# Attention state kept per half of a sequence, outputs as rounded high and low products, and level scores of two blocks in alternation

## The reference, cut to what matters

```
x = h @ up_w.T ; shift = silu(conv4(x)) ; q, k, g, tau = projections of shift
v = sigmoid(x @ ig_w1.T @ ig_w2.T + ig_b2) * x
it = softplus(g)**sigmoid(tau) ; rt_log = -softplus(g) * sigmoid(tau)
kn = k / max(|k|, 1e-12) * it
# for tokens t:  S_t = diag(exp(rt_log_t)) S_(t-1) + kn_t^T v_t ;  o_t = q_t S_t
o = scan(q / 8, kn, v, rt_log) + shift * residual_weight
xg = o * silu(h @ gate_w.T) ; o = xg * rsqrt(mean(xg*xg) + eps) * norm_weight
return o @ down_w.T
```

## Time and profile before

| what | value |
|---|---|
| median of 3 runs | 2241.48 us (2240.04 to 2248.97) |
| span of the profiled execution | 2240.6 us |
| PE busy | 2160.7 us, 96% of the span, 17266 matmul records |
| PEld (weight loads) | 2042.4 us, 91% |
| DVE busy | 1544.0 us, 69%, 4162 instructions |
| ACT busy | 1197.9 us, 53%, 2399 instructions |
| POOL busy | 92.0 us, 4% |
| mean granted TensorE clock | 0.997 of 2.4 GHz |
| DMA | mean 16 GB/s; near idle after the first slice of 40 |

### The profile page before, as it was taken

How to read it: one execution, slowest core, us unless ns; L and a number is a source line. 1 busy time by engine, 2 the same in 40 slices (tenths; PEclk the granted TensorE clock), 3 DMA queues, 4 the chain that set the end, 5 groups by cost and what they waited for, 6 DMA issues and landing times.

```text
span 2240.6 us, 46115 instructions
## 1 busy us (share of the span) xinstructions
PE 2160.7 (96%) x17266; PEld 2042.4 (91%) x17266; DVE 1544.0 (69%) x4162; ACT 1197.9 (53%) x2399; POOL 92.0 (4%) x103
## 2 busy tenths in 40 slices
PE   1999999999999999999999999999999999999999
PEld 1999989999899998999989899998999989999998
DVE  6777667777667676666766677776767766667665
ACT  5565545555455564455645455554555545556453
POOL 0000000000000000000000000000000000000000
PEclk9999999999999999999999999999999999999999
DMA  7000000000000000000000000000000000000000
GB/s 272 1 11 11 11 12 1 11 11 11 12 6 6 12 11 12 11 2 11 11 12 11 7 6 11 11 11 12 1 11 12 11 11 11 1 11 11 11 6 6
DMA packets 23441, 34.96 MB, mean 16 GB/s; under 512 B 2946, under 2 KB 19714, under 8 KB 23187
## 3 DMA queue, kind: packets, MB, share of 16 engines
q1 hardware_dynamic: 23186, 31.46, 4.2%
HBM read 23.07 MB, written 8.39 MB: 14 GB/s over the span
## 4 chain that ended last, share of the span: by engine, by line
PE 95%; issue 3%; SPq 0%; ACT 0%; DVE 0%; DMA 0%; POOL 0%; POOLq 0%; DVEq 0%; ACTq 0%
PE fb L316 59%; PE ab L316 17%; PE ab L487 4%; PE ab L500 4%; PE ab L503 3%; PE ab L508 3%; PE ab L438 1%; PE ab L428 1%; PE ab L366 1%; PE ab L480 1%; PE fb L549 0%; ACT wwhole L597 0%; SPq L225 0%; DMA small<-stage_w 0%; PE ab L478 0%
## 5 line engine op out<-in xcount | busy, mean ns | idle before, releaser
L316 PE MATMUL fb<-hid1h,wwhole 128*128 128x256 f32 x2048 | 501.8, 286 | 0.0
L316 PE MATMUL fb<-hid1l,wwhole 128*128 128x256 f32 x2048 | 488.1, 279 | 0.0
L316 PE MATMUL fb<-hid0l,wwhole 128*128 128x256 f32 x2048 | 483.8, 279 | 0.0
L316 PE MATMUL fb<-hid0h,wwhole 128*128 128x256 f32 x2048 | 483.8, 279 | 0.0
L697 ACT ACTIVATE raw<-fb,sh_s 128x256 f32<-128x256 f32 x512 | 213.6, 468 | 449.6 <-PE fb L316 345.7
L316 PEld LDWEIGHTS fb<-hid1h,wwhole 128*128 128x128 f32 x2048 | 384.0, 187 | 56.3 <-issue 51.9
L316 PEld LDWEIGHTS fb<-hid1l,wwhole 128*128 128x128 f32 x2048 | 384.3, 188 | 0.0
L316 PEld LDWEIGHTS fb<-hid0h,wwhole 128*128 128x128 f32 x2048 | 384.1, 188 | 0.0
L316 PEld LDWEIGHTS fb<-hid0l,wwhole 128*128 128x128 f32 x2048 | 384.1, 188 | 0.0
L997 DVE SCALAR_TENSOR_TENSOR shift<-shift,resw_s,ab 128x128 f32<-128x128 f32 x256 | 71.9, 343 | 267.0 <-PE ab L503 202.5
L316 PE MATMUL fb<-xnth,wwhole 128*128 128x256 f32 x1024 | 239.3, 277 | 0.0
(11 more groups left out here) (179 smaller groups left out, 4472.4 us busy)
## 6 DMA issues: line engine op xcount, KB each, us to landing
xin<-x SPq DMA_DIRECT2D x32, 256.0 KB, 2.7
out<-xin SPq DMA_DIRECT2D x32, 256.0 KB, 2.3
stream<-stage_w SPq DMA_DIRECT2D x6, 512.0 KB, 7.2
sgate<-stage_w SPq DMA_DIRECT2D x4, 512.0 KB, 4.3
shift<-stage_w SPq DMA_DIRECT2D x4, 512.0 KB, 5.2
v<-stage_w SPq DMA_DIRECT2D x4, 512.0 KB, 5.5
raw<-stage_w SPq DMA_DIRECT2D x3, 512.0 KB, 6.0
mixed<-stage_w SPq DMA_DIRECT2D x3, 512.0 KB, 8.4
```

What stands on the lines that cost most here:

```text
L316: mm = pe.matmul(o, a, b, start=start and i == 0, stop=stop and i == len(pairs) - 1)
```

## The change

The state is no longer updated after each block of 128 tokens but once per sequence, at the end of the first half, and it is read once, in the second half. What the second block of a half needs of the first comes as a "cross" score block of 128x128 (`atth[:, 1, :]`), a product of `kx` (decayed k of block 0) with the decayed q of block 1. So the outputs of a half are one set of products: v of block 0 with [own scores | cross scores] (256 columns), v of block 1 with its own scores (128 columns), and in the second half the state with the decayed q of both blocks (256 columns).

All operands of these products are now split: ScalarE writes the high parts of v (`vh`, in the place of `parth`), of the cross block, of the decayed k (`kdh`), of the scores (`atth`) and of the state (`stateh`), VectorE the low parts. The products are fp32r with 128 rows. The state products take `qhl`, which has the high part of q in rows 0 to 63 and the low part in rows 64 to 127, against a state that is held twice.

The norms block gets a second product with `pair_ones` (the sum of q*k, `qk_sum`) in the place of `own`; the transposes run in first halves only. The level scores of both blocks are issued together, block 0 and block 1 in turn, ahead of h2; the break in the middle of h2's first tile is gone. Both output sets are issued after quarter b = 2, in first halves behind the state update. On VectorE both `masked` come together, the third quarter of `hidden_low` behind them and the fourth behind the seven additions.

The diff, cut to its core (most of the lines that it removes are left out here; they stand in the listing above):

```diff
+        atth, attl = sb("atth", [P, 3, CH], F32R), sb("attl", [P, 3, CH], F32R)
+        stateh, statel = sb("stateh", [P, DI], F32R), sb("statel", [P, DI], F32R)
+        kdq = sb("kdq", [P, 2, N], F32R)
+        kdh, kdl = (kdq[:, i, :].rearrange("p (c a k) -> p c a k", c=NC, a=2) for i in range(2))
+        qhl = kdq[:, 0, :]
...
+        kx, qs = bsum[rows(1), :], small[rows(0), 4:6, :]
...
@@ tensor engine @@
-                            if name == "h2" and m == 0 and k == FB // 2:
-                                level_scores(1)
...
                 pe.wait_ge(qk_ev.sem, qk_ev.at(me))
                 pe.wait_ge(tanh_d.sem, tanh_d.at(me, 2))
+                pe.wait_ge(score_d.sem, score_d.at(me))
+                if p == 0:
+                    pe.transpose(ab[2][:, 0:P], t5, ident_s[:]).then_inc(kt_mm.sem, 1)
                 pe.matmul(ab[3][:, N:N + NC], t4, pair_ones[:], start=True, stop=True)
...
+                pe.matmul(ab[3][:, N + NC:N + 2 * NC], qk, pair_ones[:], start=True, stop=True)
+                pe.matmul(ab[3][:, 0:CH], kx, t1[rows(1), :], start=True, stop=True).then_inc(dg_mm.sem, 1)
+
+                pe.wait_ge(v_d.sem, v_d.at(me))
+                pe.wait_ge(levq_d.sem, levq_d.at(me))
+                pe.wait_ge(levk_d.sem, levk_d.at(me))
+                for i in range(LEVELS):
+                    for c in range(NC):
                         mm = pe.matmul(ab[c][:, i * UP:(i + 1) * UP], lev[rows(c), i, :], levq[rows(c), i, :], start=True, stop=True)
+                mm.then_inc(lv_mm.sem, 1)
+
+                def state_update():
...
+                    pairs = []
+                    for c in range(NC):
+                        hi, lo = (t[:, c, :, :].rearrange("p a k -> p (a k)") for t in (kdh, kdl))
+                        pairs += [(hi, vh[:, c, :]), (hi, vl[:, c, :]), (lo, vh[:, c, :])]
+                    wide(ab[3][:], pairs).then_inc(su_mm.sem, 1)
+
+                def outputs():
...
                     for d in range(DB):
+                        o = ab[d // 2][:, (d % 2) * N:(d % 2 + 1) * N]
+                        cols = slice(d * P, (d + 1) * P)
+                        first = [(vh[:, 0, cols], atth[:, 0:2, :]), (vh[:, 0, cols], attl[:, 0:2, :]), (vl[:, 0, cols], atth[:, 0:2, :])]
+                        if p == 1:
+                            first += [(stateh[:, cols], qhl), (statel[:, cols], qhl)]
+                        wide(o, first, stop=False)
+                        mm = wide(o[:, CH:N], [(vh[:, 1, cols], atth[:, 2, :]), (vh[:, 1, cols], attl[:, 2, :]),
+                                               (vl[:, 1, cols], atth[:, 2, :])], start=False)
+                        if d % 2 == 1:
+                            mm.then_inc(ot_mm.sem, 1)
                 for b in range(4):
                     pe.wait_ge(gelu1_d.sem, gelu1_d.at(me, 2 * b + 2))
                     hidden("h2", b, hid1h, hid1l, h2_mm, hid1_hi, hid1_lo)
-                    if b in (1, 2):
-                        outputs(b - 1)
+                    if b == 2:
+                        if p == 0:
+                            state_update()
+                        outputs()
...
@@ scalar engine @@
+                act.wait_ge(v_d.sem, v_d.at(me))
+                act.activation(vh, v[:], ACT.Copy).then_inc(vhi_d.sem, 1)
...
+                if p == 1:
+                    act.wait_ge(qs_d.sem, qs_d.at(seq))
+                    act.activation(qhl[rows(0), :].rearrange("p (c t) -> p c t", c=NC), qs, ACT.Copy).then_inc(q_hi.sem, 1)
...
+                act.activation(atth[:, 1, :], ab[3][:, 0:CH], ACT.Copy, scale=rkn[:, 0:1]).then_inc(cross_hi.sem, 1)
+                if p == 0:
+                    for c in range(NC):
+                        act.activation(kdh[:, c, :, :], ab[2][:, c * K:(c + 1) * K].unsqueeze(1).to_broadcast([P, 2, K]), ACT.Copy,
+                                       scale=rkn[:, c:c + 1]).then_inc(kd_hi.sem, 1)
...
+                    if b == 0:
+                        act.wait_ge(att_d.sem, att_d.at(me))
+                        act.activation(atth[:, 0:3:2, :], att[:], ACT.Copy).then_inc(att_hi.sem, 1)
+                    if b == 2 and p == 0:
+                        act.wait_ge(su_mm.sem, su_mm.at(seq))
+                        act.activation(stateh[:], ab[3][:], ACT.Copy).then_inc(st_hi.sem, 1)
...
@@ vector engine @@
-                dve.tensor_tensor(t5, k_s, t5, ALU.mult).then_inc(kd_d.sem, 1)
+                dve.tensor_tensor(kx, k_s[rows(0), :], t5[rows(0), :], ALU.mult).then_inc(kx_d.sem, 1)
                 dve.tensor_tensor(t1, q_s, t1, ALU.mult).then_inc(qd_d.sem, 1)
+                if p == 0:
+                    dve.tensor_tensor(qk, q_s, k_s, ALU.mult)
+                    dve.wait_ge(kx_d.sem, kx_d.at(me))
+                    dve.scalar_tensor_tensor(t5, k_s, later_k[:], t5, ALU.mult, ALU.mult).then_inc(score_d.sem, 1)
+                else:
+                    dve.tensor_tensor(qk, q_s, k_s, ALU.mult).then_inc(score_d.sem, 1)
+                    dve.wait_ge(qd_d.sem, qd_d.at(me))
+                    dve.tensor_scalar(qs[:, 0, :], t1[rows(0), :], 1.0, None, ALU.mult)
+                    dve.tensor_scalar(qs[:, 1, :], t1[rows(1), :], earlier_q[rows(1), :], None, ALU.mult).then_inc(qs_d.sem, 1)
...
                 def masked(c):
-                    dve.wait_ge(lv_mm.sem, lv_mm.at(me, c + 1))
+                    dve.wait_ge(lv_mm.sem, lv_mm.at(me))
                     dve.scalar_tensor_tensor(mprod[:, c, :, :].rearrange("p l u -> p (l u)"), ab[c][:, 0:LEVELS * UP], rkn[:, c:c + 1],
                                              masks_s[:].rearrange("p l u -> p (l u)"), ALU.mult, ALU.mult).then_inc(mask_d.sem, 1)
                 hidden_low(hid1l, hid1h, 0, hid1_hi, hid1_lo)
+                dve.wait_ge(vhi_d.sem, vhi_d.at(me))
+                low(vl, v[:], vh).then_inc(vlo_d.sem, 1)
+                if p == 1:
+                    dve.wait_ge(q_hi.sem, q_hi.at(seq))
+                    low(qhl[rows(1), :].rearrange("p (c t) -> p c t", c=NC), qs,
+                        qhl[rows(0), :].rearrange("p (c t) -> p c t", c=NC)).then_inc(q_lo.sem, 1)
                 dve.wait_ge(dg_mm.sem, dg_mm.at(me))
+                dve.tensor_copy(qk_sum[:], ab[3][:, N + NC:N + 2 * NC])
                 dve.tensor_scalar(ssk[:], ab[3][:, N:N + NC], KEPS2, None, ALU.max).then_inc(ss_d.sem, 1)
                 hidden_low(hid1l, hid1h, 1, hid1_hi, hid1_lo)
+                dve.wait_ge(ss_d.sem, ss_d.at(me))
                 dve.wait_ge(rkn_d.sem, rkn_d.at(me))
                 for c in range(NC):
-                    dve.scalar_tensor_tensor(att[:, c, :], own(c), rkn[:, c:c + 1], ident_s[:], ALU.mult, ALU.mult).then_inc(att_d.sem, 1)
+                    dve.tensor_scalar(att[:, c, :], ident_s[:], rkn[:, c:c + 1], qk_sum[:, c:c + 1], ALU.mult, ALU.mult).then_inc(att_d.sem, 1)
                 masked(0)
+                masked(1)
                 hidden_low(hid1l, hid1h, 2, hid1_hi, hid1_lo)
-                hidden_low(hid1l, hid1h, 3, hid1_hi, hid1_lo)
-                masked(1)
+                dve.wait_ge(cross_hi.sem, cross_hi.at(me))
+                dve.scalar_tensor_tensor(attl[:, 1, :], ab[3][:, 0:CH], rkn[:, 0:1], atth[:, 1, :].bitcast(F32), ALU.mult,
+                                         ALU.subtract).then_inc(cross_lo.sem, 1)
+                if p == 0:
+                    dve.wait_ge(kd_hi.sem, kd_hi.at(seq))
+                    for c in range(NC):
+                        dve.scalar_tensor_tensor(kdl[:, c, :, :], ab[2][:, c * K:(c + 1) * K].unsqueeze(1).to_broadcast([P, 2, K]),
+                                                 rkn[:, c:c + 1], kdh[:, c, :, :].bitcast(F32), ALU.mult, ALU.subtract).then_inc(kd_lo.sem, 1)
                 dve.wait_ge(mask_d.sem, mask_d.at(me))
                 for i in range(LEVELS):
                     m = CH >> (i + 1)
                     dve.wait_ge(att_d.sem, att_d.at(me, NC + i))
                     upper = att[:].rearrange("p c (b u r) -> p c b u r", u=2, r=m)[:, :, :, 1, :]
                     dve.tensor_tensor(upper, upper, mprod[:, :, i, :].rearrange("p c (b r) -> p c b r", r=m), ALU.add).then_inc(att_d.sem, 1)
+                hidden_low(hid1l, hid1h, 3, hid1_hi, hid1_lo)
+                dve.wait_ge(att_hi.sem, att_hi.at(me))
+                low(attl[:, 0:3:2, :], att[:], atth[:, 0:3:2, :]).then_inc(att_lo.sem, 1)
...
+                    dve.wait_ge(st_hi.sem, st_hi.at(seq))
+                    low(statel[:], ab[3][:], stateh[:]).then_inc(st_lo.sem, 1)
```

More of the change, by code:

```diff
@@ L143, in layer_program @@
         msq, rms = sb("msq", [P, NC]), sb("rms", [P, NC])
[L144 to L145 removed]
+        nbt, later_k, earlier_q = sb("nbt", [P, 1]), sb("later_k", [P, 1]), sb("earlier_q", [P, 1])
+        qk_sum = sb("qk_sum", [P, NC])
         fb = [ctx.enter_context(nc.psum_tensor(f"fb{i}", [P, 512], F32)) for i in range(4)]
@@ L190, in layer_program @@
         e2, odd = att[:, 0, :], att[:, 1, :]
+        qk = att[:, 0, :]
```

(36 more changed lines are left out.)

103 lines of the change are left out of this document (61 added, 42 removed).

## The result

The changed kernel takes 2294.35 us (median of 4 runs, 2294.09 to 2295.59) against 2242.19 us of the kernel before (4 runs, 2240.04 to 2248.97): a ratio of 1.0235, 95% interval 1.0223 to 1.0248. The profiled execution has a span of 2292.6 us, 52.0 more than before, and a mean granted clock of 0.953 where it was 0.997.

The account below looks back on a forecast made before the run. The prediction took TensorE's instruction stream to bound the kernel, busy 96% of the span. From 2240.6 us it took 167 of work, added 145 of waits and 36 of slower clock: 2255 us, 8-in-10 range 2203 to 2290.

Parts of the forecast that it names:

- What TensorE loses and gains: TensorE's attention work around h2 (scores, state update, outputs) falls from 377 to 210 us, a saving of 167 us.
- narrow fp32r matmuls cost 0.21: Rival: the 128-column output matmuls take 0.21 us each, not 0.12, adding 35 us for 2290 us; chance 0.11.
- What is late next: TensorE waits twice a half in h2 for VectorE's third and fourth low parts of the hidden layer, 145 us in all.
- The clock: TensorE's clock drops to 1.2 GHz for one 3.4 us stretch in nearly every half, losing 36 us in all.
- an end, 98 us: Upper end of the clock term: two low stretches of 3.4 us a half, 32 x 3.0 us.
- The sum: Whole kernel: profiled span 2240.6 less 167 of work, plus 145 of waits and 36 of clock, 2255 us.
- likeliest case: The forecast itself for the whole kernel: 2255 us, own range 2235 to 2276, chance 0.60.
- clock holds: Rival: TensorE's clock stays up through the waits, 2219 us, or 2205 with shorter waits; chance 0.17.

Follow-up runs that it names:

- early_all: Changed kernel with VectorE reordered: third and fourth hidden_low early, low parts of v and q last, ScalarE's q copy later; 2085.70 us, ratio 0.9313 to the kernel before.
- x1_last_early: Changed kernel with the fourth hidden_low moved right behind the third, ahead of the level additions; 2177.54 us, ratio 0.9726 to the kernel before.
- one_wait: Changed kernel with the third hidden_low right behind the second and the fourth behind the third level addition; 2211.60 us, ratio 0.9846 to the kernel before.
- early_series: early_all with level scores in series, block 0's seven and then block 1's, not alternating; 2140.76 us, ratio 0.9554 to the kernel before.
- early_split: early_all with block 0's level scores ahead of h2 and block 1's in the middle of its first block; 2130.82 us, ratio 0.9511 to the kernel before.
- fourth_mid3: Changed kernel with the fourth hidden_low behind the third of seven level additions, not the seventh; 2246.84 us, ratio 1.0033 to the kernel before.
- before_pairs: Kernel before with both blocks' level scores alternating ahead of h2, and third and fourth hidden_low early on VectorE; 2187.53 us, ratio 0.9761.
- x2_third_early: Changed kernel with the third hidden_low moved right behind the second, the fourth left in place; 2282.14 us, ratio 1.0188 to the kernel before.
- fourth_mid5: Changed kernel with the fourth hidden_low behind the fifth of seven level additions, not the seventh; 2278.97 us, ratio 1.0165 to the kernel before.
- before_late: Kernel before with only the fourth hidden_low moved behind the seven level additions; 2422.11 us, ratio 1.0804.

## Why the prediction failed, point by point

- **What TensorE loses and gains: right.** -167 forecast, -164 by the account, -166 between the spans of before and early_all. The score block was 2.57 forecast and measured. The state update runs from 947.32 to 948.71, 1.39 us (1.42 forecast), and 24 output matmuls from there to 951.40, 2.7 us (2.86). The rival "narrow fp32r matmuls cost 0.21" is dead:

```profile
947.32 0.40 PE L351 MATMUL ab<-parth,kdq 128*128 128x512 f32 x1
...
948.71 0.28 PE L351 MATMUL ab<-atth,parth 128*128 128x256 f32 x1
948.83 0.28 PE L351 MATMUL ab<-attl,parth 128*128 128x256 f32 x1
948.95 0.28 PE L351 MATMUL ab<-atth,partl 128*128 128x256 f32 x1
949.07 0.23 PE L351 MATMUL ab<-atth,parth 128*128 128x128 f32 x1
949.13 0.27 PE L351 MATMUL ab<-attl,parth 128*128 128x128 f32 x1
949.24 0.27 PE L351 MATMUL ab<-atth,partl 128*128 128x128 f32 x1
949.35 0.33 PE L351 MATMUL ab<-atth,parth 128*128 128x256 f32 x1
```

Six take 0.64 to 0.68 us; with the wide ones at 0.118 a narrow one costs 0.10 to 0.11, a little under the 0.12 that the forecast took for its floor. The Trainium skill (TensorE: Matmul & The Clock Gate, Back-to-back issue gap) has about 0.08; the trace doesn't reach it in fp32r.
- **What is late next: right.** Two waits, 1.40 and 2.83 us in first halves (1.42 and 3.08 forecast), 151 us in all for 145. In second halves they were 2.34 and 1.8 to 2.2 (2.0 and 2.5 forecast): `ssk` began 2.0 us after the score block there (995.57 to 997.59) and not 1.7 to 1.8, which moves time from the second wait to the first.
- **"The clock": the step that failed, by its size.** It read: "I expect one such stretch in nearly every half", 36 us. There were two in 31 of 32 halves, 6.8 us, and the clock cost 67 us more than before. The one stretch was taken from the loop's return, where the clock fell at 191.20 and TensorE worked again at 191.60, 0.40 us later. The waits here go on longer after the fall: 1.47 of the first 3.41 low microseconds in the half above are idle. By the forecast's own times TensorE does four steps of work between S + 3.5 and S + 8.5, so a clock that falls in there falls into idling. I let a part of the one stretch lie in the wait, and did not ask whether a wait that goes on behind the fall brings a second stretch. Two stretches stood in the text only as an end, 98 us; that end charged 3.0 us a half, and they cost 2.1, because idle time at the low clock loses nothing.
- **The sum.** The forecast of 2255 with the clock at 67 and the waits at 151 is 2292, the measured span. The mechanism was the likeliest case's; the size of one term, the clock's 36 us, was off by 31, and the waits' 6 and the work's 3 came on top.
- **The rival "clock holds"** fell in this kernel: mean clock 0.953. It holds where only the shorter wait is left, in the first halves of x1_last_early: 16 waits with starts 1.7 us apart, no fall behind any.

## What to carry to other kernels

When a change takes work off the bounding engine, list what the other engines must now deliver earlier and put their short, urgent outputs ahead of their long, patient ones; here one line's place on VectorE was worth 117 us, and the order in all 209, more than the 164 us of the change itself. Price a new wait on TensorE twice, once as idle time and once as the low clock behind it, and ask whether the wait still runs when the clock has fallen. Judge such a change only after the other engines' lists have been put in order for it: the same arithmetic was 2.35% slower and 6.9% faster.

## What the runs showed of the hardware

- Apart from a program's last one, nearly every low stretch was 3.4 us long or 6.8. In the seven kernels with waits I went through all that began in or behind a wait: 67 were of 3.4 us, and in them TensorE worked again when the clock fell or soon after (0.35 us in the rows above); 132 were of 6.8 us, and in them it idled through more of the first 3.41 us (1.47 and 1.57 in the rows above). No short one idled as long in its first 3.41 us as any of the long ones.
- Whether the clock falls at all behind a wait is not settled by the wait's length alone: it fell behind 13 of 16 waits with starts 2.6 us apart in x1_last_early, and failed to fall behind 5 of 16 with starts 3.1 us apart in one_wait.
- The clock also fell without any wait. In early_series it fell in 11 of 32 halves with no idle time before it, between 0.24 us before and 0.65 us after the start of the last of the 28 narrow passes (64 rows by 64 columns) in series; PE windows around one:

```profile
345.20:348.61 3.41, 3.41 (x38) 1.00 0.02 5
348.61:352.00 3.39, 3.39 (x16) 0.50 0.00 0
352.00:355.40 3.40, 3.40 (x31) 1.00 0.00 0
```

PE shows as busy in all three, since its ends are modelled. The kernel before has two groups of 14 such passes, with h2 steps between, and no fall behind them; early_split, with the same two groups in the changed kernel, has none either. Which of length, width or row group does it was not tried.
- Loop returns, with starts 1.9 to 2.5 us apart, brought a low stretch in 3 of 15 cases before, in none in the changed kernel, fourth_mid3 and early_all, in 2 to 8 in before_pairs, x2_third_early, fourth_mid5, before_late, early_split and x1_last_early, in 10 in one_wait and 11 in early_series. Executions of one kernel differ as well (2198 to 2224 us in one_wait, with mean clocks of 0.981 to 0.970), and I can't say from these runs what decides it.
